# Pair products of a recommendation model: 64-row pairs of matmuls against zero-padded full-height matmuls

## What is computed

```python
emb = emb_tables[jnp.arange(26)[:, None], x_cat]          # 26 x 2048 x 64
emb = jnp.transpose(emb, (1, 0, 2))
dense_embed = price[:, None] @ Wp + bp                    # 2048 x 64
feats = jnp.concatenate([emb, dense_embed[:, None, :]], axis=1)
gram = jnp.einsum('bid,bjd->bij', feats, feats)           # 2048 x 27 x 27
interactions = gram[:, _IU, _JU]                          # 351 pairs
h = relu(dense_embed @ W1 + b1)
dense_out = relu(h @ W2 + b2)
t = relu(concatenate([interactions, dense_out], 1) @ Wt1 + bt1)
out = (t @ Wt2 + bt2)[:, 0]
```

## Time and profile before

| | us |
|---|---|
| median of 3 runs | 543.34 |
| lowest and highest run | 540.46 and 543.46 |
| the profiled execution | 542.15 |
| its span | 540.3 |

### The profile page before, as it was taken

The page is one execution under the profiler, slowest core; times in us unless marked ns, Lnnn a source line. Parts: engine busy times, 40 slices in busy tenths (PEclk is TensorE's granted clock), DMA queues, the critical chain, the costliest instruction groups (busy, mean ns, idle before and its releaser), DMA issues.

```text
span 540.3 us, 4362 instructions
## 1 busy us (share of the span) xinstructions
PE 246.3 (46%) x1496; PEld 177.9 (33%) x1496; DVE 145.4 (27%) x358; ACT 169.1 (31%) x405; POOL 393.8 (73%) x425
## 2 busy tenths in 40 slices
PE   0118033240569515134249733315136960565775
PEld 0105033240534304133234423305134440544654
DVE  3003233040331504123040331503233051333353
ACT  0124323041241604223042440503224052243563
POOL 6777777777777777777777777777777777777750
PEclk9999665555659856555577975755555985669798
DMA  6233333333323333333333333333332333332210
GB/s 187 26 26 27 26 28 27 26 27 27 26 27 27 26 27 28 26 26 27 26 29 26 27 27 26 27 27 27 26 27 26 26 28 26 26 28 27 28 22 2
DMA packets 14360, 16.26 MB, mean 30 GB/s; under 512 B 7169, under 2 KB 7425, under 8 KB 14209
## 3 DMA queue, kind: packets, MB, share of 16 engines
q0 software_dynamic: 13312, 13.66, 30.9%
q1 hardware_dynamic: 578, 2.19, 1.1%
q10 hardware_dynamic: 448, 0.14, 0.1%
HBM read 15.95 MB, written 0.01 MB: 30 GB/s over the span
## 4 chain that ended last, share of the span: by engine, by line
POOL 68%; issue 26%; DMA 2%; PE 2%; ACT 1%; DVE 0%; POOLq 0%
POOL gathered L200 68%; DMA gathered<-in_table,row_idx 2%; PE ps_mlp L487 1%; ACT gram L141 1%; PE ps_trans L419 1%; DMA raw_idx<-in_x_cat 0%; POOLq L50 0%; PE ps_gram L456 0%; PE ps_mlp L479 0%; PE ps_mlp L495 0%; DVE feats L166 0%; DVE top L368 0%; ACT scores L279 0%; DVE row_idx L339 0%; DVE wrapped L332 0%
## 5 line engine op out<-in xcount | busy, mean ns | idle before, releaser
L200 POOL DMA_INDIRECT gathered<-in_table,row_idx x416 | 392.7, 944 | 128.0 <-issue 125.9
L419 PE MATMUL ps_trans<-ident,gathered 128*128 128x128 f32 x208 | 45.4, 381 | 223.0 <-DMA gathered<-in_table,row_idx 223.0
L456 PE MATMUL ps_gram<-feats 64*128 64x128 f32 x1024 | 105.2, 384 | 61.0 <-ACT gram L141 30.2
L141 ACT COPY gram<-ps_gram 32x112 f32<-32x112 f32 (+1 forms) x272 | 97.2, 357 | 108.1 <-PE ps_gram L456 105.2
L141 DVE COPY gram<-ps_gram 32x112 f32<-32x112 f32 (+1 forms) x272 | 96.6, 355 | 116.8 <-PE ps_gram L456 113.5
L456 PEld LDWEIGHTS ps_gram<-feats 64*128 64x128 f32 x1024 | 96.9, 286 | 75.4 <-issue 52.6
L419 PEld LDWEIGHTS ps_trans<-ident,gathered 128*128 128x128 f32 x208 | 35.0, 198 | 236.3 <-issue 234.9
L151 ACT COPY feats<-ps_trans 64x448 f32<-64x448 f32 (+1 forms) x60 | 34.1, 569 | 195.4 <-PE ps_trans L419 195.0
L151 DVE COPY feats<-ps_trans 64x448 f32<-64x448 f32 (+1 forms) x60 | 36.8, 613 | 203.3 <-PE ps_trans L419 202.7
L487 PE MATMUL ps_mlp<-gram,wt1p_sb 128*128 128x512 f32 (+2 forms) x168 | 60.2, 520 | 2.9 <-ACT gram L141 2.9
L487 PEld LDWEIGHTS ps_mlp<-gram,wt1p_sb 128*128 128x128 f32 x168 | 32.6, 228 | 32.6 <-issue 28.0
(11 more groups left out here) (24 smaller groups left out, 33.5 us busy)
## 6 DMA issues: line engine op xcount, KB each, us to landing
gathered<-in_table,row_idx POOLq DMA_INDIRECT x416, 3.3
price_bc<-in_price SPq DMA_DIRECT2D x1, 1024.0 KB, 5.2
wt1p_sb<-in_wt_pairs SPq DMA_DIRECT2D x1, 896.0 KB, 7.8
raw_idx<-in_x_cat SPq DMA_DIRECT2D x1, 195.0 KB, 2.7
w_sb<-in_w ACTq DMA_DIRECT2D x2, 32.0 KB, 4.8
wt1d_sb<-in_wt_dense ACTq DMA_DIRECT2D x1, 64.0 KB, 7.7
raw_idx<-in_x_cat SPq DMA_DIRECT2D x1, 13.0 KB, 1.8
consts_sb<-in_consts ACTq DMA_DIRECT2D x1, 4.5 KB, 2.0
```

What stands on the lines that cost most here:

```text
L141: last = copy(gram_to[QUAD * c:QUAD * (c + 1), n % 2, t - BATCHES[n][0], :, rg * r:rg * (r + 1), :, s], source[QUAD * s:QUAD * (s + 1), :, ...
L200: pool.indirect_dma_start(out=gathered[:, to * D:(to + 1) * D], out_offset=None, in_=rows, in_offset=bass.IndirectOffsetOnAxis(ap=row_idx[ ...
L419: last = nc.tensor.transpose(ps_trans[:, to + k * P:to + (k + 1) * P], gathered[:, base + f * D:base + (f + 2) * D], ident[:, :])
L456: last = nc.tensor.matmul(ps_gram[:, out_at:out_at + P], group, group, start=True, stop=True)
```

## The change

ScalarE gets a new step, `pad_halves`, between its copy of chunk 1 and the evacuation of round 0. It copies `feats` into a new buffer `padded`, which has 256 columns per group: partitions 0 to 63 go to the first 128 columns and partitions 64 to 127 to the last 128, and the rest stays at the zeros of a new memset. A round of a tile other than the last is then 8 matmuls in place of 16: the group of all 128 partitions of `feats` is the stationary operand and the 256 columns of `padded` move. Because of the zeros, the first 128 result columns are the lower half's products and the last 128 the upper half's. Round 0 and round 1 wait for the two copies in place of the three semaphores of before. In PSUM the two halves of a group now lie side by side. The last tile's four rounds are as they were, written in place.

```diff
+        padded = sb("padded", [P, GROUPS, 2 * P])
...
+        padded_made = sem("padded_made")
...
-        gram_from = ps_gram[:, :].rearrange("p (h g s j c) -> p h g s j c", h=2, g=RG, s=GROUP, j=PAD // GROUP, c=GROUP)
+        gram_from = ps_gram[:, :].rearrange("p (g h s j c) -> p h g s j c", h=2, g=RG, s=GROUP, j=PAD // GROUP, c=GROUP)
...
-            act.wait_ge(feats_zeroed, 1)
+            act.wait_ge(feats_zeroed, 2)
...
+            def pad_halves(t):
+
+                act.wait_ge(trans_evac_dve, NC * (t + 1))
+                act.wait_ge(trans_evac_act, NC * (t + 1))
+                act.wait_ge(dense_slot_set, 2 * (t + 1))
+                for h in range(2):
+                    nc.scalar.copy(padded[D * h:D * (h + 1), :, P * h:P * (h + 1)],
+                                   feats[D * h:D * (h + 1), :, :].rearrange("p (g s) j -> p g (s j)", s=GROUP))\
+                        .then_inc(padded_made, 1)
...
                 odd_fields(1, t)
+                pad_halves(t)
                 if first and n > 0:
                     store_scores(n - 1)
...
             nc.vector.memset(feats[:, :, :], 0.0).then_inc(feats_zeroed, 1)
-            dve.wait_ge(feats_zeroed, 1)
+            nc.vector.memset(padded[:, :, :], 0.0).then_inc(feats_zeroed, 1)
+            dve.wait_ge(feats_zeroed, 2)
...
-            def gram_matmuls(first, groups, to, apart):
-
-                for g in range(groups):
-                    for h in range(2):
-                        at = (first + g) * GROUP
-                        group = feats[D * h:D * (h + 1), at:at + GROUP, :].rearrange("p s j -> p (s j)")
-                        out_at = to + h * apart + g * P
-                        last = nc.tensor.matmul(ps_gram[:, out_at:out_at + P], group, group, start=True, stop=True)
-                return last
-
             def gram_round(t, r):
-                wait_trans_evac(NC * (t + 1))
-                pe.wait_ge(dense_slot_set, 2 * (t + 1))
+                pe.wait_ge(padded_made, 2 * (t + 1))
                 wait_gram_evac(ROUNDS * t + r)
-                gram_matmuls(RG * r, RG, 0, 2 * BANK).then_inc(gram_done, 1)
+                for g in range(RG):
+                    at = RG * r + g
+                    last = nc.tensor.matmul(ps_gram[:, 2 * P * g:2 * P * (g + 1)], feats[:, GROUP * at:GROUP * (at + 1), :],
+                                            padded[:, at, :], start=True, stop=True)
+                last.then_inc(gram_done, 1)
...
```

More of the change, by code:

```diff
@@ L472, in gram_last @@
                 wait_gram_evac(ROUNDS * LAST + max(r - 1, 0))
-                gram_matmuls(LAST_RG * r, LAST_RG, 2 * BANK * (r % 2), BANK).then_inc(gram_done, 1)
+                for g in range(LAST_RG):
+                    for h in range(2):
+                        at = (LAST_RG * r + g) * GROUP
+                        group = feats[D * h:D * (h + 1), at:at + GROUP, :].rearrange("p s j -> p (s j)")
+                        to = 2 * BANK * (r % 2) + h * BANK + g * P
+                        last = nc.tensor.matmul(ps_gram[:, to:to + P], group, group, start=True, stop=True)
+                last.then_inc(gram_done, 1)
             def top_layer(n):
```

## The result

| | before | changed |
|---|---|---|
| median of 6 runs each, us | 542.81 | 547.62 |
| lowest and highest | 540.46 and 543.93 | 547.16 and 552.52 |
| the profiled execution, us | 542.15 | 547.52 |
| its span | 540.3 | 545.7 |

The changed kernel takes 1.0112 times as long (95% interval 1.007 to 1.0154): slower. By the medians it is 4.8 us (0.9%), about half of the 9.0 that were forecast. Its 547.62 lies inside the stated range of 547 to 558, by 0.6 us at its lower edge. The forecast took a difference under 1% for no change; on which side of that this one lies, the interval leaves open.

A forecast was written before the change was run, and what follows sets the result against it. GpSimd's gathers bound the kernel (520 of 540.3 us). Tile 14's copies 3.8, round 0 3.3 and round 1 2.45 make 9.6, less 0.65 swallowed: 9.0; 542.15 + 9.0 = 551.15, the median 1.2 higher: 552.3 us, range 547 to 558.

The forecast's parts named there:

- Where it is decided: Tile 14, whose rounds stand in front of the last tile, alone decides the change; 9.6 us there, 9.0 on the span.
- The copies: ScalarE's two copies before round 0 of tile 14: 1.90 us each, 3.8 us together, all on the chain.
- Round 0: Tile 14's first gram round: 5.4 us, part slow and part fast clock, in place of 2.06; adds 3.3.
- Round 1: Tile 14's second gram round: 5.4 us at the middle clock in place of 2.95; adds 2.45.
- What the waits for the last gathers swallow: Near the end, TensorE's 0.65 us wait for the last gather absorbs delay, leaving 9.0 of 9.6 us.
- The end: From the last transpose to the end of the span: some 15.5 us, as now.
- The other tiles: Tiles other than 14 cost nothing; tile 5's first transposes end at 195.5, 2.9 us to spare before a gather.
- The rival of stalls: GpSimd stalls mid-kernel after tiles 4 and 8, perhaps 12: some 553, 556 to 558, or 566 to 573 us; chance 0.21.
- The price of a padded round: A new gram round of 16 records takes 3.76 us at the full clock, 7.0 at the half clock.
- The rival with rounds at their old price: Gram rounds keep their length as row pairs don't really overlap; only the copies cost, 3.2 us, 546.5; chance 0.07.
- Start and memset: At the start, a second memset of 3.5 us, hidden by VectorE's 17.35 us wait for its first transposes.
- The rival of the clock staying high: Both tile 14 rounds take 3.76 us: 549.0, or 547.6 if the last tile's top layer also quickens; chance 0.18.

The follow-up runs named there:

- tile 14 in pairs: Changed kernel with tile 14 back in the old row pairs, tiles 0 to 13 in the new form; 542.23 against 542.05 us before, 1.001.
- tile 14 alone padded: Changed kernel with tiles 0 to 13 back in the old form, only tile 14 in the new one; 549.86 us, 1.0154 of the kernel before.
- copies only: Changed kernel with ScalarE's two copies and the wait for them, but the rounds of the kernel before; 547.49 us, 1.012 of the kernel before.
- columns only: Changed kernel without the copies, its 256-column matmuls reading unpadded features, so products differ from the reference; 545.97 us, 1.0078 of the kernel before.
- changed, fillers: Changed kernel plus 7 useless keep-warm matmuls before tile 14's round 0 and 5 between its rounds; 547.61 against 542.08 us before, 1.012.
- changed, copies on two engines: Changed kernel with the upper half's copy moved from ScalarE to VectorE; 555.74 against 542.08 us before, 1.0238.
- the first two kernels: The runs tile 14 in pairs and tile 14 alone padded, against the kernel before; 1.001 and 1.0154.
- the order of halves: Kernel before with each round's lower-half matmuls first, then the upper-half ones, instead of by turns; 670.03 against 658.57 us on that chip, 1.0165.

## Why the prediction was right, and where its size was off

The prediction had the place and the direction right, and its size about twice too large. The table has the chain of tile 14 for the kernels on the undisturbed chips, each from the timeline of TensorE, in us.

| kernel | round 0 starts, takes | round 1 takes | last tile's first rounds start | span |
|---|---|---|---|---|
| before | 495.12, 2.06 | 2.95 | 516.94 | 540.3 |
| changed | 499.24, 5.41 | 3.69 | 524.91 | 545.7 |
| tile 14 in pairs | 495.69, 2.06 | 2.06 | 517.94 | 541.3 |
| tile 14 alone padded | 498.94, 6.58 | 5.07 | 526.99 | 547.7 |
| copies only | 499.01, 3.79 | 3.79 | 523.26 | 543.8 |
| columns only | 496.24, 4.88 | 5.38 | 521.37 | 545.2 |
| changed, fillers | 499.45, 3.72 | 3.69 | 524.84 | 545.6 |
| changed, copies on two engines | 504.88, 5.11 | 5.38 | 533.09 | 553.8 |

- **Where it is decided.** Right: tile 14 alone, shown by the first two kernels.
- **The copies.** Forecast 3.8, measured 3.82 in one row; round 0 starts 4.12 us later, 0.3 of it because the tile's transposes were late.
- **Round 0.** Forecast 5.4, measured 5.41, as a mean between the clock's two levels; that it came so near is luck, as the other padded kernels had 3.72 to 6.58.
- **Round 1.** Forecast 5.4, measured 3.69 at 1.00 of the clock: 1.7 us too much. This is one of the two mis-sized terms. With the gap between the rounds (-0.2) and the stretch after them (-0.1), the chain is 4.12 + 3.35 + 0.74 - 0.24 = 7.97 us late, where 9.6 was forecast.
- **What the waits for the last gathers swallow.** Forecast 0.65, measured 1.04 (7.97 to 6.93): besides the wait that the earlier trace rows has, the transposes before it had waited too, and the last rounds 0.25 for a copy of VectorE (the row at 525.79 above).
- **The end.** Forecast "some 15.5 us from the last transpose, as now". It is 13.9 (531.75 to 545.7); behind the last tile's last rounds the loss shrinks by 1.53 (6.93 to 5.4). This is the other mis-sized term, and the larger error of thought: I gave the clock a price in tile 14 only, and a gain in the last tile's top layer (1.4) only in a rival. The stage of the last top layer, at 0.87 of the clock before, ran at 1.00. In all, 9.0 less 1.6 on the chain, 0.4 in the waits and 1.5 at the end leaves 5.5, and the span grew by 5.4.
- **The other tiles.** Hidden, as taken. The value that I chose for tile 5's transposes was 195.5 and they ended at 195.7. That this fits so well is luck: it took 5.4 us for each of tile 3's rounds, which took 6.25 and 6.61, and 3.76 for each of tile 4's, which took 5.41 and 3.69. A faster top layer between them and a shorter delay by the copies made up for it. Besides, GpSimd waited 1.5 us in all for transposes, none of which moved its last gather. The rival of stalls didn't come.
- **The price of a padded round.** 3.76 warm forecast, 3.69 measured; 7.0 cold, 6.62 at most measured. The reason given, two halves side by side, is borne out by the order of halves. The rival with rounds at their old price is ruled out.
- **Start and memset.** 3.47 us at 8.81, and the first copy of VectorE comes at 25.63: hidden.

The rival of the clock staying high (549.0, or 547.6 with the top layer quick; chance 0.18) gave the better time, and the second figure is the measured median. By its mechanism it was half right, for round 1 and the end; round 0 took 5.41 where it has 3.76, so its hit is partly luck as well.

## What to carry to other kernels

Filling the rows of the array by padding the other operand with zeros gained nothing here, where pairs of half-height matmuls already ran side by side: it doubles the columns and adds the copies. Ask first whether neighbours in the queue use different halves of the array. Where a chain with idle gaps sets the end, price its clock up to the last instruction. Measure the whole chain after a gain early in it: with the fillers and with the copies on two engines, what was won at tile 14's round 0 was lost again before the last tile's first rounds.

## What the runs showed beyond that

- A VectorE copy between SBUF tiles of 64 x 2048 in 1.24 us makes the gather beside it 1.72 us in place of 0.94; in the whole run the longest takes 1.98. A memset of 128 x 4096 on VectorE (3.47 us) left the gathers at 0.94.
- Idle time alone, without one more matmul, lengthened two later rounds from 2.06 and 2.95 to 3.79 each (the kernel with copies only; granted clock 0.50 in both).
- The order of two loops, lower half and upper half, is worth 6.50 against 3.79 us a round at the half clock.
- The same kernel took 542, 655 and 659 us on different chips, by waits that its own trace can't name.
